# A third of the weights' low halves made by VectorE from the loaded piece, and new orders on all queues

## The reference

```python
x = x + causal_attention(layernorm(x), W_qk, W_v, alibi)        # one head
x = x + cross_attention(layernorm(x), ctx, wq, wk, wv, wfc)     # 16 heads of 16
x = x + ffn(layernorm(x), w_gate, w_gate_up, w_down)
def ffn(x):                        # D = 256, F = 1024, E = 8 experts, 2 per token
    p = softmax(x @ w_gate); keep the two largest of 8, divide by their sum
    g, u = split(einsum('bsd,edh->ebsh', x, w_gate_up))
    return sum over e of p[e] * ((silu(g) * u) @ w_down[e])
```

## Time and profile before

| | |
|---|---|
| runs | 1071.54, 1072.26, 1072.60 us |
| profiled execution | 1069.32 us, its span 1067.5 us |
| granted TensorE clock, mean | 0.983 |
| TensorE busy | 998.5 us, 94% |
| TensorE busy from 546 to 1067 us | 511.4 of 521 us |
| VectorE, ScalarE, GpSimd busy | 60%, 59%, 50% |
| chain that ended last | TensorE 75%, VectorE 7%, issue 5%, DMA 4%, ScalarE 4%, GpSimd 3% |

### The profile page before, as it was taken

One profiled execution on the slowest core, in us unless ns is written; L12 is line 12 of the kernel. 1 busy time (PEld: TensorE's weight loads), 2 busy tenths in 40 slices (PEclk: granted clock), 3 DMA queues, 4 the chain that ended last, 5 costly groups with the idle time before them and its releaser, 6 DMA issues.

```text
span 1067.5 us, 36427 instructions
## 1 busy us (share of the span) xinstructions
PE 998.5 (94%) x12720; PEld 833.8 (78%) x12720; DVE 641.9 (60%) x2082; ACT 628.5 (59%) x1343; POOL 537.4 (50%) x582
## 2 busy tenths in 40 slices
PE   5689999999999999967989999999999999999996
PEld 4356666666666666635989999999999999999886
DVE  6677888888888888863566444444444444444333
ACT  6589898888888888855343333333333333333332
POOL 6856777777777777623344332232332323333342
PEclk9799999999999999998999999999999999999999
DMA  6855665667666565359744555962654753335552
GB/s 195 258 181 161 181 184 191 198 198 197 182 178 202 162 190 175 112 120 310 198 69 61 144 92 151 275 176 50 173 162 106 224 159 62 48 51 168 165 153 24
DMA packets 146247, 167.74 MB, mean 157 GB/s; under 512 B 75008, under 2 KB 123200, under 8 KB 141824
## 3 DMA queue, kind: packets, MB, share of 16 engines
q1 hardware_dynamic: 130910, 148.66, 46.3%
q0 software_dynamic: 15248, 18.18, 10.5%
q10 hardware_dynamic: 18, 0.01, 0.0%
HBM read 270.75 MB, written 43.07 MB: 294 GB/s over the span
## 4 chain that ended last, share of the span: by engine, by line
PE 75%; DVE 7%; issue 5%; DMA 4%; ACT 4%; POOL 3%; SPq 1%; DVEq 0%; ACTq 0%; POOLq 0%
PE front L2744 16%; PE t_ring L2744 15%; PE pv L2774 7%; PE s_ring L2774 7%; PE pv L2521 5%; PE s_ring L2488 4%; PE t_ring L2506 3%; PE front L2371 3%; PE front L2362 3%; PE front L2421 2%; PE tail L2371 2%; POOL w_halves L905 1%; DMA xn_t<-xn_h 1%; DVE nmax L1580 1%; DMA rows<-normed,row_i 1%
## 5 line engine op out<-in xcount | busy, mean ns | idle before, releaser
L1004 POOL DMA_INDIRECT out<-y_sb,place_i x64 | 100.5, 1571 | 281.0 <-DVE y_sb L2117 109.1
L2744 PE MATMUL front<-rows_t,wgu_sb 128*128 128x128 f16 x3072 | 195.0, 221 | 2.2 <-DVE act_t L2124 1.6
L2744 PE MATMUL t_ring<-rows_t,wgu_sb 128*128 128x128 f16 x3072 | 192.6, 219 | 0.0
L2744 PEld LDWEIGHTS front<-rows_t,wgu_sb 128*128 128x128 f16 x3072 | 184.9, 99 | 6.0 <-issue 2.2
L2744 PEld LDWEIGHTS t_ring<-rows_t,wgu_sb 128*128 128x128 f16 x3072 | 182.4, 98 | 3.4 <-issue 0.6
L1177 ACT ACTIVATE probs_t<-t_ring,mask_bias 128x512 f32<-128x512 f32 x256 | 164.4, 699 | 15.9 <-PE t_ring L2506 11.7
L1580 DVE TENSOR_REDUCE nmax<-s_ring 128x2 f32<-128x512 f32 x256 | 165.3, 683 | 13.0 <-PE s_ring L2488 10.7
L1338 ACT ACTIVATE silu_g<-t_ring 128x256 f32<-128x256 f32 x136 | 51.8, 383 | 156.2 <-PE t_ring L2744 141.6
L2124 DVE SCALAR_TENSOR_TENSOR act_t<-t_ring,silu_g 128x256 f32<-128x256 f32 x136 | 57.6, 424 | 142.6 <-ACT silu_g L1338 142.2
L1338 ACT ACTIVATE silu_g<-front 128x256 f32<-128x256 f32 x136 | 52.0, 384 | 153.9 <-PE front L2744 141.9
L2124 DVE SCALAR_TENSOR_TENSOR act_t<-front,silu_g 128x256 f32<-128x256 f32 x136 | 57.7, 424 | 127.9 <-ACT silu_g L1338 127.5
(11 more groups left out here) (314 smaller groups left out, 1860.9 us busy)
## 6 DMA issues: line engine op xcount, KB each, us to landing
wgu_sb<-gu_split SPq DMA_DIRECT2D x68, 2048.0 KB
wd_sb<-down_split SPq DMA_DIRECT2D x68, 1024.0 KB
w_piece<-in_w_gu SPq DMA_DIRECT2D x32, 512.0 KB, 6.6
gu_split<-w_halves SPq DMA_DIRECT2D x32, 512.0 KB, 3.8
w_piece<-in_w_down SPq DMA_DIRECT2D x16, 512.0 KB
down_split<-w_halves SPq DMA_DIRECT2D x16, 512.0 KB, 4.4
x_in<-in_x SPq DMA_DIRECT2D x16, 256.0 KB, 2.9
ctx_in<-in_ctx_t_in SPq DMA_DIRECT2D x16, 256.0 KB, 3.2
```

The source lines that it names most:

```text
L1004: nc.gpsimd.indirect_dma_start(out=out, out_offset=bass.IndirectOffsetOnAxis(ap=place_i[:, j:j + 1], axis=0), in_=y_sb[:, j], in_offset=No ...
L2744: o = nc.tensor.matmul(gu_ring[f][:, part * SLOT:(part + 1) * SLOT], wgu_sb[j][:, w, at:at + P], rows_t[:, j, NC * r + c], start=(i == 0), ...
```

## The change

For piece i = 2 of each three (`BY_VECTOR = (2,)`) ScalarE writes only the high half. The low half is made by VectorE in one scalar_tensor_tensor over 1024 columns, piece times scale minus high half, read from `w_piece` itself. GpSimd makes the low halves of pieces 0 and 1 only. `piece_split` becomes `piece_lo` (GpSimd's) and `piece_rest` (VectorE's); SP waits for both before it stores, and for VectorE's before it loads into the same buffer. Beside that the calls in `iteration` and `first_fronts` stand in another order on all five engines; the ending is the same.

```diff
+        BY_VECTOR = (2,)
+        BY_POOL = CHUNKS - len(BY_VECTOR)
 SP, load_pieces:
                     sp.wait_ge(piece_hi, CHUNKS * (b - 1))
+                    sp.wait_ge(piece_rest, len(BY_VECTOR) * (b - 1))
 SP, store_pieces:
-                sp.wait_ge(piece_split, CHUNKS * b + CHUNKS)
+                sp.wait_ge(piece_lo, BY_POOL * b + BY_POOL)
+                sp.wait_ge(piece_rest, len(BY_VECTOR) * b + len(BY_VECTOR))
 SP, iteration:
                     store_stream(b - 1)
-                    transpose_normed(b - 1, 1 - p)
                 if f and (not isinstance(b, int) or b + 4 < B):
                     load_next(b + 4, p)
+                if c:
+                    transpose_normed(b - 1, 1 - p)
                 if f:
                     store_pieces(b + 2, h + 1, p)
                     stack_rows(b + 2, p)
                     stack_k_hi(b + 2, p)
+                    stack_k_lo(b + 2, p)
                 if s and f:
                     stack_max(b + 1, 1 - p)
                 if f:
-                    stack_k_lo(b + 2, p)
 GpSimd, iteration:
                 if f:
+                    ctx_rest(b + 2)
                     xn_rest(b + 2)
-                    ctx_rest(b + 2)
                 if parted:
                     scatter_first(b - 2, p, h + p - 1)
                     scatter_part(p, 1)
+                    scatter_part(p, 2)
...
-                if parted:
-                    scatter_part(p, 2)
-                    scatter_part(p, 3)
+                if n:
+                    rsqrt_norm1(b + 3)
                 if c:
                     xn3_rest(b - 1, 1 - p)
-                if n:
-                    rsqrt_norm1(b + 3)
                 if f:
-                    split_lo(b + 2, 2)
                     rsqrt_norm2(b + 2)
+                    xn2_rest(b + 2)
                 if n:
                     f_norm1(b + 3, 1 - p)
-                if f:
-                    xn2_rest(b + 2)
+                if parted:
+                    scatter_part(p, 3)
 ScalarE, split_hi:
-                nc.scalar.activation(w_halves[:, i, 0], w_piece[:, p, i], ACT.Copy, scale=WSCALE)
+                halves = nc.scalar.activation(w_halves[:, i, 0], w_piece[:, p, i], ACT.Copy, scale=WSCALE)
+                if i in BY_VECTOR:
+                    halves.then_inc(piece_hi, 1)
+                    return
 ScalarE, iteration:
                 if f:
+                    f_ctxt(b + 2, p, h + 1)
                     f_xnt(b + 2)
-                    f_ctxt(b + 2, p, h + 1)
...
                 if t:
+                    h_exp(b, 2, 1)
                     h_exp(b, 3, 0)
+                if f:
+                    split_hi(b + 2, 2, p, h + 2)
+                if t:
                     h_exp(b, 3, 1)
                 if c:
                     t_xn3(b - 1, 1 - p, h + p - 1)
-                if t:
-                    h_out(b, p, 0)
-                if f:
-                    split_hi(b + 2, 2, p, h + 2)
...
+                    f_q(b + 2, 1 - p, h + p + 1)
                 if s:
                     h_max(b + 1)
-                if f:
-                    f_q(b + 2, 1 - p, h + p + 1)
 VectorE:
+            def split_lo(k, i, p):
+                vec.wait_ge(piece_hi, CHUNKS * k + i + 1)
+                vec.sem_inc(vec_passed, 1)
+                nc.vector.scalar_tensor_tensor(w_halves[:, i, 1], w_piece[:, p, i], WSCALE, w_halves[:, i, 0],
+                                               ALU.mult, ALU.subtract).then_inc(piece_rest, 1)
 VectorE, iteration:
                     f_stats2(b + 2)
                     f_aggr2(b + 2)
+                    split_lo(b + 2, 2, p)
                     f_var2(b + 2)
                 if s:
                     h_max(b + 1, 9, 11)
+                if f:
+                    f_norm2(b + 2)
...
                 if s:
                     h_max(b + 1, 15, 16)
                 if c:
+                    t_sum_recip(b - 1)
                     t_probs(b - 1)
...
-                    t_gates(b - 1, 1 - p)
-                    t_rows(b - 1, 1 - p)
                     t_chosen(b - 1)
-                    t_rank(b - 1)
-                    t_pick(b - 1)
-                    t_pos(b - 1)
                 if f:
                     f_q(b + 2)
                 if c:
+                    t_gates(b - 1, 1 - p)
+                    t_rows(b - 1, 1 - p)
+                    t_rank(b - 1)
+                    t_pick(b - 1)
+                    t_next_row(b - 1)
+                    t_pos(b - 1)
                     t_pos_i(b - 1, 1 - p)
-                    t_next_row(b - 1)
```

More of the change, by code:

```diff
@@ L1225, in iteration @@
                 if f:
-                    split_hi(b + 2, 1, p, h + 2)
+                    f_q1(b + 2)
+                    f_k(b + 2, 1 - p, h + p + 1)
+                if c:
+                    t_ont(b - 1)
                 if t:
@@ L1288, in first_fronts @@
                 gate_hi()
+                f_q1(0)
                 f_xnt(1)
+                f_v1(0)
                 f_probs(0)
-                f_v1(0)
+                f_ctxt(1, 1, 0)
+                f_probs_t(0)
                 f_v2(0, 0)
-                f_probs_t(0)
-                f_ctxt(1, 1, 0)
+                f_q1(1)
                 split_hi(0, 0, 0, 1)
                 split_hi(0, 1, 0, 1)
-                f_q1(1)
+                f_probs(1)
                 split_hi(0, 2, 0, 1)
+                f_xn2t(0)
                 f_k(1, 0, 1)
-                f_xn2t(0)
-                f_probs(1)
+                f_probs_t(1)
+                f_v2(1, 1)
                 f_v1(1)
-                f_probs_t(1)
                 f_q(0, 1, 0)
-                f_v2(1, 1)
                 split_hi(1, 0, 1, 1)
@@ L1820, in iteration @@
                     t_gate_max(b - 1)
-                if f:
-                    f_norm2(b + 2)
-                if c:
                     t_shift(b - 1)
@@ L1929, in first_fronts @@
                 f_stats2(0)
+                f_scores(1)
                 f_aggr2(0)
+                f_row_max(1)
                 f_var2(0)
+                f_sums(1)
+                f_norm2(0)
                 f_stats1(2, 0, 1)
-                f_norm2(0)
-                f_scores(1)
-                f_row_max(1)
+                split_lo(0, 2, 0)
                 f_k(1)
@@ L1938, in first_fronts @@
                 f_var1(2)
-                f_sums(1)
+                f_q(0)
                 f_attn(1, 1)
-                f_q(0)
                 f_stats2(1)
@@ L2584, in iteration @@
                 if f:
+                    f_k(b + 2)
                     f_q1(b + 2)
@@ L2647, in iteration @@
                 if t:
-                    h_scores_t(b, p, 6, 0)
+                    h_scores_t(b, p, 7, 1)
                 if c:
                     t_gate(b - 1)
-                if t:
-                    h_scores_t(b, p, 6, 1)
-                    h_values(b, p, 5)
+                if f:
+                    f_xn2t(b + 2)
                 if s:
                     h_scores(b + 1, q, h + p, 12, 14)
-                if f:
-                    f_xn2t(b + 2)
                 if t:
-                    h_scores_t(b, p, 7, 0)
-                    h_scores_t(b, p, 7, 1)
+                    h_values(b, p, 6)
+                    h_values(b, p, 7)
                 if s:
                     h_scores(b + 1, q, h + p, 14, 15)
-                if t:
-                    h_values(b, p, 6)
+                if f:
+                    f_q(b + 2)
                 if s:
@@ L2668, in iteration @@
                     f_v2(b + 2)
-                if t:
-                    h_values(b, p, 7)
+                    f_q_rest(b + 2)
                 if s:
                     h_max(b + 1)
-                if f:
-                    f_q(b + 2)
-                    f_q_rest(b + 2)
                 if c:
@@ L2684, in first_fronts @@
                 f_k(0)
+                f_k_rest(0)
                 f_q1(0)
-                f_k_rest(0)
                 f_q1_rest(0)
+                f_v1(0)
                 f_scores(0)
-                f_v1(0)
                 f_xnt(1)
                 f_v2(0)
+                f_q1(1)
                 f_probs_t(0)
-                gate_ready()
+                f_q1_rest(1)
+                f_k(1)
                 f_attn(0)
-                f_q1(1)
-                f_k(1)
+                f_scores(1)
+                f_xn2t(0)
                 f_k_rest(1)
                 f_v2(1)
-                f_q1_rest(1)
-                f_scores(1)
-                f_xn2t(0)
+                f_probs_t(1)
+                gate_ready()
+                f_q(0)
                 f_v1(1)
-                f_probs_t(1)
-                f_q(0)
                 f_q_rest(0)
```

124 lines of the change are left out of this document (64 added, 60 removed).

## The result

| | before | after |
|---|---|---|
| runs, median and span of them | 1072.5 us (1071.5 to 1072.6, five) | 1083.4 us (1082.1 to 1085.3, five) |
| profiled execution, its span | 1069.3, 1067.5 us | 1082.1, 1080.4 us |
| granted TensorE clock, mean | 0.983 | 0.981 |
| TensorE, VectorE, ScalarE, GpSimd busy | 94%, 60%, 59%, 50% | 92%, 61%, 57%, 46% |

The ratio is 1.0106, 95% interval 1.0092 to 1.0120: slower by 11 us. The forecast of 1080 and its sign hold: 1083.4 lies in its range of 1076 to 1085. Its reasons mostly do not, and that is what this part is about.

A forecast was written before the change was run, and what follows sets the result against it. TensorE's order was taken as the bound. Per iteration -1.3 + 0.8 + 1.26 + 0.9 - 0.88 = +0.8 us: +9.4 for twelve, -0.7 first and last, -0.5 start-up, total +8.2, forecast 1080; range 1064 to 1087, its own 1076 to 1085.

The forecast's parts named there:

- Rival 1: Attention loop: VectorE and GpSimd don't shut each other out at these places; -0.5 us an iteration, 1065 us, chance 0.31.
- The sign: Iteration's end: t_rank following the last projection within 0.7 us would mean the forecast is wrong and rival 1 holds.
- E + 0.95: Next iteration's start if the gate chain is unhindered, 0.95 us after E, the end of TensorE's last projection.
- (a): Middle of the iteration: ScalarE loses one copy ahead of the exponentials, so TensorE waits less; -1.3 us an iteration.
- (b): Second norm: VectorE's new scalar_tensor_tensor stands ahead of f_var2 and TensorE waits before f_xn2t; +0.8 us an iteration.
- (c): Iteration's end: GpSimd's f_norm1 holds up VectorE's gate operations, so TensorE waits for t_rank; +1.26 us, unhindered +0.6.
- X: Time mark in the iteration: the end of TensorE's f_xn2t, from which the gate chain's times are counted.
- (d): Next iteration's beginning: GpSimd's ctx_rest holds up t_pick, t_ont waits +0.9 us, replacing the start's lost 0.88.
- (e): SP's queue: transpose_normed, k_lo and store_pieces in new places or with new waits; costed at nothing.
- (f): Start-up to 57 us: GpSimd does one piece less, VectorE's split stands among row maxima; -0.5 us, bounds -2.0 to +1.2.

The follow-up runs named there:

- y_split_alone: On y_before: only VectorE's split of the third piece and what it replaces, all orders those of before; 1085.2 us, ratio to before 1.0061.
- y_after: The changed kernel with its two transposing transfers replaced by plain copies; 1094.4 us, ratio to before 1.0128.
- w_probe: Separate kernel without the computation: seven VectorE operations beside GpSimd idle, tensor_scalar or tensor_tensor; a series took 5.5 us beside tensor_tensor instead of 1.83.
- y_before: The kernel before with its two transposing transfers replaced by plain copies; 1073.1 us, ratio to before 0.9947.
- y_start: On y_after: start-up of all five queues in the order of before, splits where y_split_alone has them; 1093.8 us, ratio to before 1.0122.

## Why the prediction was right, and where it was not

The number came out right by errors that cancel: the sum had +9.4 for twelve iterations, -0.7 for the first and last, -0.5 for the start-up. Measured are -0.3 for the seven ordinary iterations, +7.4 for b = 0 to 3 and 11 to 14 together, +6.8 in the start-up and -1.0 behind. That the sum comes near is luck. Rival 1's case was the one that held inside the iteration: gprob and gden were undisturbed. The sign that I had set for it, t_rank within 0.7 us behind the projection, was not met: t_rank starts at 262.43, 0.95 behind the projection's end by steps (261.48), and 1.3 were forecast. The sign was set too tight, since my own unhindered schedule has E + 0.95. Rival 1's time, 1065, was far off all the same: neither it nor the forecast counted SyncE's queue or the start-up.

- **(a) ScalarE's missing copy, -1.3.** Right in sign and place, mis-sized. The middle loses 0.42 us by steps instead of 1.09, and 0.23 behind it where before lost 0.15: -0.6.
- **(b) The split on VectorE, +0.8 at f_xn2t.** Its duration was right: 1.23 us against 1.27 estimated, step 1.14 against 1.15. Under the old orders it cost +0.65 an iteration (y_split_alone), by way of the row maxima, not of f_xn2t. The step that failed is its clearance: I followed only the chain to f_norm2 and not what else is queued behind the split on its engine. In after TensorE has no such wait, though the split is there as well; its new order has the scores 11 and 12 further back. The chain to f_norm2 itself was sized right there: from x_res at 250.04 to the end of f_norm2 at 256.32 are 6.28 us, 6.3 forecast. f_xn2t (256.39) doesn't wait for it because TensorE needed 6.67 us instead of my 6.0 to get there, having lost the 0.42 of the middle and 0.23 in front of the gate. An estimate from these: without the two losses it would wait some 0.6, so what (a) could still gain, (b) would take. That the new orders pay for the split in the ordinary iteration is inferred, from 28.11 against 28.15 on one side and 28.8 against 28.16 on the other; no run shows it by itself, since y_after didn't repeat the changed kernel's iteration.
- **(c) f_norm1 shuts out the gate chain, t_rank +1.26.** Wrong. gprob took 0.17 and gden 0.14 inside it; the two caught operations lost 0.25 and 0.16, overlapping, 0.17 on the chain, and w_probe has at most 0.21 beside a tensor_scalar. chosen ends 5.49 us behind X, where I had 5.36 unhindered and 6.0 hindered. TensorE waits 0.57 us for it (0.73 by steps), the +0.6 that the text gave as unhindered. I had carried rows of GpSimd's tensor_tensor over to its tensor_scalar. The Trainium skill (SBUF — State Buffer, section Who interferes with whom) has the two-input VectorE instruction contend with any GpSimd instruction that reads SBUF; for VectorE's small operations beside tensor_scalar the measurement differs (0.21 us at most), and so it does for the split, which kept its 1.21; beside tensor_tensor it agrees (1.10 us instead of 0.16), and so does GpSimd's wait for the split (up to 1.05 us).
- **(d) ctx_rest shuts out t_pick and pos_i, t_ont +0.9 for -0.88.** Half right. t_pick slipped in ahead of ctx_rest (235.24 and 235.63), the cast of pos_i was caught for 0.9 us as told, and t_ont still didn't wait: the second o_n was there at 238.92, 0.7 us ahead of it. The start's 0.88 shrank to 0.45 by steps. What came in their place is (e).
- **(e) SyncE's queue, cost nothing.** This is the step that failed worst. TensorE's first two scores of the next entry moved ahead of f_scores, from 8.0 to 6.6 us behind the mark, and need q_lo, which lands there: 0.4 to 0.5 us by steps in an ordinary iteration, and no slack left. Late issues of SyncE then reach TensorE: one issue of a q tile took 1.35, 2.50 and 2.54 us instead of 0.60 in b = 3, 11 and 13, and the scores waited 0.73, 1.83 and 1.42, where the ordinary wait is at most 0.36. The transposed rows made t_gate wait 1.87 and 0.59; nmax_t 3.48 instead of 1.83 in the last. I named covers for nmax_t and t_gate, and none for q_lo. Before has long issues as well (q_lo took 1.68, 1.62 and 1.69 us in b = 2, 11 and 12), and its scores, placed behind f_scores, never waited more than 0.7; these iterations took 28.46, 28.15 and 28.39 us. That the moved scores let the late issues through is argued from these rows: no run puts the scores back. Why SyncE stalls in b = 11 and 13 (the first and the third iteration behind the loop's end) isn't shown.
- **(f) Start-up, -0.5, bounds -2.0 to +1.2.** Outside its bounds: +6.8. 3.9 are the two splits (y_split_alone), a term that I had as 1.15 against up to 2.56 gained on GpSimd; no such gain shows in y_split_alone. The whole 6.8 splits by first copies into three: 4.2 from y_before to y_after, 1.4 from y_after to after (62.16 to 63.58), and 1.1 that y_before's start-up is itself behind before's (57.93 and 56.80). The 1.4 can be seen in after: weight_rest's first w_split took 2.33 us, beside GpSimd's ctx_rest and its affine selects (10.66 to 12.43), where y_after's took 0.68, and f_scores(0) comes at 21.98 instead of 20.23; 1.4 of these 1.75 us are left at the copy. The orders are the same, so this collision is one that a small shift makes or unmakes. The 1.1 lie between two kernels with the same orders; 0.7 of them are there at the first k_lo (17.03 and 17.74), and their cause isn't shown. The granted clock takes part: its mean over the start-up is 0.88 in before and y_before, 0.86 in y_split_alone and y_start, 0.81 in after and y_after. What that costs by itself isn't shown, since y_start and y_after have the same first copy.

The two rows of that collision, after and y_after:

```profile
10.65 2.33 DVE L1883 SCALAR_TENSOR_TENSOR w_split<-w_scaled,w_split 128x512 f16<-128x512 f32 x1
```
```profile
10.49 0.68 DVE L1883 SCALAR_TENSOR_TENSOR w_split<-w_scaled,w_split 128x512 f16<-128x512 f32 x1
```

The terms I could have had from the trace of before are (e) and (f): the earlier trace rows showed a stretch paced by VectorE, and anything put among the row maxima there is paid in full.

Not tried are the new orders without the data change, f_norm1 ahead of xn2_rest again, and the scores back behind f_scores. So the account of the single iterations rests on rows alone, and that of the start-up on the experiments for 3.9 to 4.2 of its 6.8 us.

## What to carry to other kernels

An operation moved onto an engine is paid where that engine's queue is already the pace (here the start-up's row maxima), and its clearance is to be read for every instruction behind it, not only for the chain it belongs to. Work of TensorE that is moved ahead takes the slack from the transfers it reads: look up when each lands, and what a late issue of its queue would do. A forecast that hits with the wrong terms teaches nothing until the marks by iteration are laid side by side; and where a single iteration is long without a longer wait, its granted clock is the next thing to read.

## What the runs showed of the hardware

- GpSimd's tensor_scalar and tensor_tensor are different neighbours. Beside tensor_tensor a VectorE operation of 0.16 us took 1.1, every second one; beside tensor_scalar none of them took more than 0.38 (w_probe), and a cast 0.42 (after). A long VectorE operation with two SBUF inputs (1.21 us) kept its time and made one GpSimd operation wait, up to 1.05 us, in w_probe. It doesn't always keep it: in the start-up of y_split_alone, amid GpSimd's splits, it took 1.69, and in that of after one of 0.68 took 2.33.
- A wait lengthened by 1.6 us cost 2.9: TensorE's granted clock was 0.57 in the 4 us behind it, where it had been 1.00 (y_before and y_split_alone, 36 to 40 us).
- The granted clock also fell in the middle of the busy loop, behind waits of 1.44 to 1.48 us of a TensorE that was busy for the rest: four iterations of y_split_alone, 1.3 to 1.8 us longer each. The same wait in the others had no such fall.
- One issue of a transfer on SyncE's queue takes 0.60 us for the q and k tiles, and now and then 1.3 to 2.5 (three of before's 45 issues of q tiles, four of after's; the longest q_lo in b = 13, 2.54).
